# Two output buffers, one move per tile and no gate operations in the expert loop of a routed feed-forward kernel

## The reference, cut to what matters

```python
weights_BSK, indices_BSK = jax.lax.top_k(probs_BSE, TOP_K)
norm_weights_BSK = jax.nn.softmax(weights_BSK, axis=-1)
full_weights_BSE = jnp.sum(one_hot_BSKE * norm_weights_BSK[..., None], axis=2)
act_BSEF = jax.nn.silu(jnp.einsum('BSD,EDF->BSEF', x, kernel_gating_EDF))
fuse_BSEF = act_BSEF * jnp.einsum('BSD,EDF->BSEF', x, kernel_up_EDF)
down_BSED = jnp.einsum('BSEF,EFD->BSED', fuse_BSEF, kernel_down_EFD)
out_BSD = jnp.einsum('BSED,BSE->BSD', down_BSED, full_weights_BSE)
```

## Time and profile before

| | us |
|---|---|
| median of 3 runs (lowest to highest) | 2512.0 (2511.35 to 2512.2) |
| the profiled execution | 2510.75 |
| its span, first to last instruction | 2509.0 |
| TensorE busy in the span | 2347.6 |
| VectorE, ScalarE, GpSimd busy | 1589.8, 1314.9, 903.4 |
| the expert stage, from the first gather to the last scatter | 2095.22 to 2491.6 |

### The profile page before, as it was taken

How to read it: one execution, slowest core, us unless ns; L and a number is a source line. 1 busy time by engine, 2 the same in 40 slices (tenths; PEclk the granted TensorE clock), 3 DMA queues, 4 the chain that set the end, 5 groups by cost and what they waited for, 6 DMA issues and landing times. The chain is left out here.

```text
span 2509.0 us, 49491 instructions
## 1 busy us (share of the span) xinstructions
PE 2347.6 (94%) x16096; PEld 2076.7 (83%) x16096; DVE 1589.8 (63%) x3452; ACT 1314.9 (52%) x3960; POOL 903.4 (36%) x1141
## 2 busy tenths in 40 slices
PE   6999999999999999999997999999999956888895
PEld 5898889888988898889886899999999844777775
DVE  5656665666566656665655788888888855334332
ACT  4555555555555555555554666666666622333332
POOL 3233333333233323333332122222222224777774
PEclk9999999999999999999999999999999986999998
DMA  5000000000000000000001000000000012334334
GB/s 166 18 10 17 8 17 8 17 9 16 8 17 14 11 8 17 16 9 9 16 1 66 3 10 18 17 8 17 17 8 17 18 37 67 77 73 97 72 49 97
DMA packets 52931, 73.89 MB, mean 29 GB/s; under 512 B 9408, under 2 KB 36800, under 8 KB 52800
## 3 DMA queue, kind: packets, MB, share of 16 engines
q1 hardware_dynamic: 39952, 55.07, 6.9%
q0 software_dynamic: 12912, 17.98, 4.4%
HBM read 55.47 MB, written 21.76 MB: 31 GB/s over the span
## 5 line engine op out<-in xcount | busy, mean ns | idle before, releaser
L356 POOL TENSOR_TENSOR p_sb<-p_sb,rinv 128x512 f32<-128x512 f32 x256 | 284.1, 1110 | 906.3 <-DVE rinv L606 906.3
L527 ACT ACTIVATE p_sb<-s_ps,nmax 128x256 f32<-128x256 f32 x512 | 238.3, 470 | 467.1 <-DVE nmax L587 441.4
L751 POOL TENSOR_TENSOR sp_sb<-sp_sb,srinv 128x512 f32<-128x512 f32 x128 | 133.4, 1042 | 442.7 <-DVE srinv L937 442.7
L462 PE MATMUL o_ps<-pt_sb,v_sb 128*128 128x128 f32 x2048 | 270.5, 275 | 1.8 <-DVE ot_lo L57 1.8
L58 DVE SCALAR_TENSOR_TENSOR qbd_lo<-m_ps,qbd_hi 64x256 fp32r<-64x256 f32 x256 | 108.1, 422 | 227.4 <-ACT qbd_hi L46 225.7
L462 PEld LDWEIGHTS o_ps<-pt_sb,v_sb 128*128 128x128 f32 x2048 | 248.7, 192 | 2.2 <-issue 2.2
L57 DVE TENSOR_TENSOR kt_lo<-k_ps,kt_hi 128x512 fp32r<-128x512 f32 x256 | 176.2, 688 | 98.1 <-ACT kt_hi L45 94.1
L45 ACT CAST kt_hi<-k_ps 128x512 fp32r<-128x512 f32 x256 | 150.6, 588 | 105.7 <-PE k_ps L65 102.7
L885 ACT ACTIVATE sp_sb<-sm_sb,snmax 128x128 f32<-128x128 f32 x512 | 199.4, 390 | 6.6 <-DVE snmax L948 3.3
L603 DVE COPY pt_sb<-t_ps 128x512 f32<-128x512 f32 x256 | 176.4, 689 | 26.5 <-PE t_ps L449 21.8
L587 DVE TENSOR_REDUCE nmax<-s_ps 128x2 f32<-128x512 f32 x256 | 174.1, 680 | 0.0
(11 more groups left out here) (278 smaller groups left out, 7711.3 us busy)
## 6 DMA issues: line engine op xcount, KB each, us to landing
ctx_raw<-in_ctx_t SPq DMA_DIRECT2D x32, 256.0 KB, 2.8
ctx_raw<-in_ctx_t SPq DMA_DIRECT2D x64, 128.0 KB, 2.9
xn<-f_xn SPq DMA_DIRECT2D x16, 256.0 KB, 2.2
acc<-x_sb SPq DMA_DIRECT2D x16, 256.0 KB, 2.3
e_raw<-in_gate SPq DMA_DIRECT2D x8, 512.0 KB, 4.1
e_raw<-in_up SPq DMA_DIRECT2D x8, 512.0 KB, 5.0
e_raw<-in_down SPq DMA_DIRECT2D x8, 512.0 KB, 6.3
x_sb<-in_x SPq DMA_DIRECT2D x1, 3584.0 KB, 13.6
```

The lines of the kernel that those rows point to most:

```text
L356: nc.gpsimd.tensor_tensor(prob, prob, inv, ALU.mult).then_inc(norm_done, 1)
L462: mm = pe.matmul(o_ps[:, (2 * w + b) * P:(2 * w + b + 1) * P], v_sb[:, k, q * P:(q + 1) * P], pt_sb[:, w, k * P:(k + 1) * P], start=(j == ...
L527: ex = nc.scalar.activation(p_sb[:, k, b * J:(b + 1) * J], s_ps[1 - w][:, b * J:(b + 1) * J], ACT.Exp, bias=nmax[:, k, b:b + 1], scale=1.0 ...
L751: nc.gpsimd.tensor_tensor(prob, prob, inv, ALU.mult).then_inc(norm_done, 1)
```

## The change

It does four things. `e_ys` becomes `ys` with two halves, used in turn by tile parity; `y_copy(i)` waits no longer for the scatter before but for `s_out_now`, the index copy of the tile before, which GpSimd makes only when the scatter two tiles before has landed. `move` is one operation of 264 columns instead of one of 8 and one of 256, `e_xs` has 264 columns, and the 8 weights go from there to `slot_weights` by a new copy on ScalarE in `step`; `move` waits for that copy of the tile before (`s_weight`). Both gate operations are dropped; in their place stands a semaphore increment on GpSimd's queue (`pool.sem_inc(s_order, 1)`), on which nobody waits, and the waits that the gate carried are carried by it. The scatters left after the loop are written as three and a rest. The waits on a scatter between `add_rows` calls stay.

```diff
--- before.py
+++ after.py
@@ -1304,31 +1304,29 @@
         with ExitStack() as ex:
             token_now = [sbuf(ex, f"e_token_now{i}", [P, 1], mybir.dt.uint32) for i in range(2)]
             warm = sbuf(ex, "e_warm", [P, 1])
-            s_warm = sem("e_silu_table")
+            s_warm, s_ready, s_order = sem("e_silu_table"), sem("e_ready"), sem("e_pool_order")
             none = sbuf(ex, "e_none", [P, 1], mybir.dt.uint32)
-            dummy = [sbuf(ex, f"e_dummy{i}", [P, 1]) for i in range(2)]
             token_out = sbuf(ex, "e_token_out", [P, 1], mybir.dt.uint32)
             xs_in = [sbuf(ex, f"e_xs_in{i}", [P, ROW]) for i in range(2)]
-            xs_sb = sbuf(ex, "e_xs", [P, D])
+            xs_sb = sbuf(ex, "e_xs", [P, ROW])
             xt_hi = sbuf(ex, "e_xt_hi", [P, D], F32R)
             xt_lo = sbuf(ex, "e_xt_lo", [P, D], F32R)
             silu_sb = sbuf(ex, "e_silu", [P, F])
             h_sb = sbuf(ex, "e_h", [P, F])
             ht_hi = sbuf(ex, "e_ht_hi", [P, F], F32R)
             ht_lo = sbuf(ex, "e_ht_lo", [P, F], F32R)
-            ys_sb = sbuf(ex, "e_ys", [P, D])
+            ys = sbuf(ex, "e_ys", [P, 2 * D])
             xt_ps = psum(ex, "e_xt_ps")
             g_ps = psum(ex, "e_g_ps")
             u_ps = psum(ex, "e_u_ps")
             ht_ps = psum(ex, "e_ht_ps")
             y_ps = psum(ex, "e_y_ps")
-            s_now, s_moved, s_dummy = sem("e_token_now_set"), sem("e_xs_moved"), sem("e_dummy_done")
+            s_now, s_moved = sem("e_token_now_set"), sem("e_xs_moved")
             s_xs, xt_mm, xt_h, xt_l = [sem(f"e_xs_loaded{i}") for i in range(2)], sem("e_xt_mm"), sem("e_xt_hi_done"), sem("e_xt_split")
             g_mm, u_mm, silu_done, h_done = sem("e_g_mm"), sem("e_u_mm"), sem("e_silu_done"), sem("e_h_done")
             ht_mm, ht_h, ht_l = sem("e_ht_mm"), sem("e_ht_hi_done"), sem("e_ht_split")
             y_mm, y_copied, s_added = sem("e_y_mm"), sem("e_y_weighted"), sem("e_ys_added")
             s_weight, s_out_now, s_out = sem("e_weight_kept"), sem("e_token_out_set"), sem("out_stored")
-            out_gate, s_out_gate = sbuf(ex, "e_out_gate", [P, 1]), sem("e_out_gate_done")
 
             def tile_count(eng):
                 return eng.value_load(first_tile[0:1, EXPERTS:EXPERTS + 1], min_val=MIN_TILES * EXPERTS, max_val=MAX_TILES)
@@ -1378,7 +1376,7 @@
                     wait(pool, s_moved, i - 1 if isinstance(i, int) else i + -1)
                     nc.gpsimd.tensor_tensor(token_now[half][:], token_of[:, bass.ds(i, 1)], none[:], ALU.add).then_inc(s_now, 1)
                     pool.wait_ge(s_now, i + 1)
-                    nc.gpsimd.tensor_tensor(dummy[half][:], zero[:], zero[:], ALU.add).then_inc(s_dummy, 1)
+                    pool.sem_inc(s_order, 1)
                     pool.indirect_dma_start(
                         out=xs_in[half][:], out_offset=None, in_=xn_dram,
                         in_offset=bass.IndirectOffsetOnAxis(ap=token_now[half][:], axis=0)).then_inc(s_xs[half], DMA)
@@ -1386,27 +1384,24 @@
                 def move(i, pair, half):
 
                     pool.wait_ge(s_xs[half], DMA * pair + DMA)
-                    wait(pool, s_dummy, i)
-                    nc.gpsimd.tensor_tensor(weight[:, bass.ds(i * EXPERTS, EXPERTS)], xs_in[half][:, D:ROW],
-                                            zero[:].to_broadcast([P, EXPERTS]), ALU.add).then_inc(s_weight, 1)
+                    wait(pool, s_weight, i)
                     wait(pool, xt_mm, i)
-                    nc.gpsimd.tensor_tensor(xs_sb[:], xs_in[half][:, 0:D], zero[:].to_broadcast([P, D]), ALU.add).then_inc(s_moved, 1)
-
-                def add_rows(i):
+                    nc.gpsimd.tensor_tensor(xs_sb[:], xs_in[half][:], zero[:].to_broadcast([P, ROW]), ALU.add).then_inc(s_moved, 1)
+
+                def add_rows(i, half):
 
                     wait(pool, s_added, DMA * i)
                     nc.gpsimd.tensor_tensor(token_out[:], token_of[:, bass.ds(i, 1)], none[:], ALU.add).then_inc(s_out_now, 1)
+                    pool.wait_ge(y_copied, i + 1)
                     pool.wait_ge(s_out_now, i + 1)
-                    pool.wait_ge(y_copied, i + 1)
-                    wait(pool, s_out_gate, i)
-                    nc.gpsimd.tensor_tensor(out_gate[:], zero[:], zero[:], ALU.add).then_inc(s_out_gate, 1)
+                    pool.sem_inc(s_order, 1)
                     pool.indirect_dma_start(
-                        out=acc, out_offset=bass.IndirectOffsetOnAxis(ap=token_out[:], axis=0), in_=ys_sb[:],
-                        in_offset=None, compute_op=ALU.add).then_inc(s_added, DMA)
+                        out=acc, out_offset=bass.IndirectOffsetOnAxis(ap=token_out[:], axis=0),
+                        in_=ys[:, half * D:(half + 1) * D], in_offset=None, compute_op=ALU.add).then_inc(s_added, DMA)
 
                 more_pairs = pool.value_load(pairs[0:1, 0:1], min_val=MIN_TILES * EXPERTS // 2, max_val=MAX_TILES // 2)
-                nc.gpsimd.memset(none[:], 0).then_inc(s_zero, 1)
-                pool.wait_ge(s_zero, 2)
+                nc.gpsimd.memset(none[:], 0).then_inc(s_ready, 1)
+                pool.wait_ge(s_ready, 1)
                 for half in range(2):
                     gather(half, half)
                 for half in range(2):
@@ -1415,17 +1410,19 @@
                 for half in range(2):
                     move(2 + half, 1, half)
                     gather(4 + half, half)
-                add_rows(0)
+                add_rows(0, 0)
                 with pool.Fori(2, more_pairs) as j:
                     for half in range(2):
                         move(2 * j + half, j, half)
                         gather(2 * j + (2 + half), half)
-                        add_rows(2 * j + (half - 3))
+                        add_rows(2 * j + (half - 3), 1 - half)
                 for half in range(2):
                     move(2 * more_pairs + half, more_pairs, half)
-                not_added = pool.value_load(first_left[0:1, 0:1], min_val=MIN_TILES * EXPERTS - 4, max_val=MAX_TILES)
-                with pool.Fori(not_added, tile_count(pool)) as i:
-                    add_rows(i)
+                left = pool.value_load(first_left[0:1, 0:1], min_val=MIN_TILES * EXPERTS - 4, max_val=MAX_TILES - 4)
+                for k in range(3):
+                    add_rows(left + k, 1 - k % 2)
+                with pool.Fori(left + 3, tile_count(pool)) as i:
+                    add_rows(i, 0)
 
             @block.tensor
             def _(pe):
@@ -1488,6 +1485,7 @@
                     act.wait_ge(xt_mm, i + 1)
                     wait(act, u_mm, i)
                     split_hi_act(nc, xt_hi[:], xt_ps[:, 0:D]).then_inc(xt_h, 1)
+                    nc.scalar.copy(weight[:, bass.ds(i * EXPERTS, EXPERTS)], xs_sb[:, D:ROW]).then_inc(s_weight, 1)
 
                 def rest(i):
 
@@ -1502,9 +1500,8 @@
 
                 def y_copy(i, e):
                     act.wait_ge(y_mm, i + 1)
-                    act.wait_ge(s_weight, i + 1)
-                    wait(act, s_added, DMA * i)
-                    nc.scalar.activation(ys_sb[:], y_ps[:, 0:D], ACT.Copy,
+                    wait(act, s_out_now, i)
+                    nc.scalar.activation(ys[:, bass.ds((i % 2) * D, D)], y_ps[:, 0:D], ACT.Copy,
                                          scale=weight[:, bass.ds(i * EXPERTS + e, 1)]).then_inc(y_copied, 1)
 
                 def tile(i, before, e, e_before, piece):
```

## The result

| | before | after |
|---|---|---|
| median of 4 runs each, us (lowest to highest) | 2512.1 (2511.35 to 2513.57) | 2534.84 (2532.41 to 2537.5) |
| ratio (95% interval) | | 1.009 (1.0073 to 1.0107) |
| profiled execution, its span | 2510.75, 2509.0 | 2537.5, 2535.8 |

The change makes the kernel 0.9% slower. The forecast was a loss, to 2526; direction and range hold, the loss is 22.7 where 14 were forecast.

What follows compares the result with a forecast made beforehand. GpSimd's loop (5.35 us a tile) and an equally long scatter loop were taken as the bound. +3.1 +11.2 -2.4 +2.6 = +14.5 on 2510.75, plus 1.25 to the median, gave 2526 us, range 2493 to 2538.

Steps and rivals of the forecast that it cites:

- The gates: Ahead of GpSimd's transfers: the increment's wait holds the queue, exposing preparation; 1.00 us instead of 0.78 before gather, 0.95 before scatter.
- One move: In GpSimd's loop, one move of all columns takes 0.64 us instead of 0.80, -0.16 a tile.
- Two buffers: The loop from one scatter to the next becomes 5.02 us, under GpSimd's 5.44, and stops being the bound.
- the sentence on which I rested the forecast: Expert stage before: removing the scatter loop (5.34 us) alone frees nothing that GpSimd's loop (5.35) does not also free.
- The ring over ScalarE: Chain from TensorE through ScalarE's new weights copy to GpSimd's move and back: 5.15 us, hidden under GpSimd's 5.44.
- Other tiles: The 34 tile periods outside the seven weight-splitting groups: each 0.09 us longer, 5.44 against 5.35, +3.1 in all.
- slow scatters: Six scatters that meet the load of weights: each costs 0.4 us less than before, -2.4 in all.
- Groups with weights: Seven groups of four tiles round splitting the next expert's weights: VectorE's e_w_lo holds GpSimd, 1.6 us each, +11.2.
- the third piece: Third e_w_lo piece in a group of tiles that split weights: it holds token_now again, 0.85 us.
- period near 7: Sign of being right: one tile per weight-splitting group with e_xs held to 2 us or more, period near 7 us.
- The end: After the last move, four scatters: the last ends at X+17.3 us, X being the last tile's e_xt_hi start; +2.6.
- The rivals: Faster, preparation hidden: 2489 us, chance 0.22; about the same, holds not adding up: 2515, 0.16; slower, ScalarE's ring: 2532, 0.12.

## Why the prediction was right, point by point

**The gates** (forecast 1.00 and 1.00 ahead of the transfers): 1.02 and 1.03, the size is right. The mechanism was not quite the one given. It was put as "a wait that holds the queue"; the increments behind the gates carry none and give the same distances. What the runs show is that an increment between the operation that the engine still has to do and the transfer takes their overlap away, and that its place decides: ahead of the gate it costs nothing or 0.06. How it does so stays open. By the Trainium skill, Perfetto Trace Analysis, section "Sequencer-only Instruction (DRAIN, etc)", the next instruction is fetched only when such an instruction has waited, executed and pushed its update. The trace agrees where the increment carries the wait: idle time ahead of the gather is 0.83 behind it and 0.36 behind a gate. The 0.59 behind an increment that waits for nothing isn't settled by it.

**One move** (-0.16): the move ends 0.67 after the scatter's descriptors instead of 0.80, -0.13.

**Two buffers** (5.02, not a bound): in the changed kernel it is none, `e_ys` waits for TensorE only. But the sentence on which I rested the forecast is wrong, as the run with two buffers alone shows: 2499, 13 us faster. I had taken 0.95 as GpSimd's own, where 0.62 is; the second buffer was worth 0.33 a tile in GpSimd's loop. The forecast survives it by luck: it set the scatter's distance at 1.00 from a tile in which `e_ys` was late, and the increment makes it 1.03 whatever `e_ys` does.

**The ring over ScalarE** (5.15, hidden): 5.16 wherever it shows, and hidden under 5.5 in the changed kernel.

**Other tiles** (34 x 0.09 = +3.1): a common tile is 5.51, where the sum gave 5.46 and 5.44 was taken: 0.02, 0.03 and 0.03 more on the two distances and the move, some 0.03 less on the scatter and the gap behind the move. The 34 take 188.49 us instead of 182.93, +5.6. The sum has a slip here: holds and slow scatters are priced over a common tile in the groups as well, so the longer common tile belongs to all 62, not to 34. That leaves out 28 x 0.09 = 2.5, and at the measured 0.16 it is 4.5.

**Groups with weights and slow scatters** (+11.2 - 2.4 = +8.8): the 28 tiles take 187.55 instead of 167.90, +19.65. These terms were mis-sized by 10.85. `token_now` is held to 0.96 and the next move to 2.17, as described. That the third piece holds `token_now` again is so in one group only, the one without a stretch at half clock; in five of the others it meets a gather instead, which takes 1.11 to 1.17. Two timeline rows of GpSimd, from the one and from one of the others:

```profile
2205.86 1.06 POOL L1377 TENSOR_TENSOR e_token_now<-token_of,e_none 128x1 uint32<-128x1 uint32 x1 [0.18 <-POOL e_xs L1389]
...
2274.10 1.12 POOL L1380 DMA_INDIRECT e_xs_in<-xn,e_token_now  x1 [0.83 <-DMA acc<-e_ys,e_token_out]
```

The "period near 7" occurs as forecast, once, at the product that comes at 2204.03: 7.28. In the other six groups the product behind the held move came after 8.76 to 8.85, because TensorE worked at half its clock, and three of the tiles behind a slow scatter took 8.57 to 8.76 for the same reason: nine stretches. "Whose clock I assume stays at 0.99" was an assumption that broke. But 8.79 against 7.28 is not the price of a stretch, since what follows gives most of it back: the three tiles together take 7.28 + 5.48 + 6.40 = 19.16 in the group without one, and 8.79 + 5.13 + 5.62 = 19.54 in that of 2264, 19.4 to 19.6 in all six. Behind a held move a stretch costs some 0.4, since it also spares the third hold. Behind a slow scatter it costs some 1.6 (8.6 to 8.8 against 6.99 and 7.20), of which the next tile gives back 0.4.

The missing 10.85 is then, by these estimates: +4.5 for the common tile of 5.51 in the 28; +2.1 for the 0.3 that the forecast took off each of the seven groups (the group without a stretch has 19.16 - 3 x 5.51 = 2.63 of holds, where 2.6 was worked out and 2.3 used); +2.2 and +4.8 for the clock behind six moves and three scatters; -2.7 since only five slow scatters lie in these tiles, where six were counted, and for rounding. The clock's part rests on one group without a stretch. The kernel with the increments behind the gates has three such groups, with 19.15 to 19.24 for the three tiles, and four with a stretch, with 19.56 to 20.62. So behind a held move a stretch costs between 0.4 and 1.4, and the clock's exact share of the loss isn't settled.

**The end** (+2.6): X + 17.35 forecast, 17.49 from the product measured, +2.73.

Together: 5.6 + 19.65 + 2.7 = 27.9, less 1.2 by which this execution reached tile 3 earlier, is the 26.75 between the profiled executions; between the medians it is 22.7.

**The rivals.** The preparation is not hidden under the increment (distances 1.02, not 0.5). The holds do add up where all three occur. ScalarE's ring is not the bound of the changed kernel, though it is once the gates are back.

## What to carry to other kernels

A tiny operation "without use" between an index and its indirect transfer can be worth more than it costs: it carries the wait inside the engine while the transfer is made ready, 0.2 us busy for 0.2 saved ahead of the gather and 0.4 ahead of the scatter here. Before pricing a loop as an engine's own, look at its gaps in a tile in which nothing is late: a gap that contains a wait for the other loop makes two loops look equally long. And where an engine is late by two microseconds, TensorE's clock may fall behind it; price that over several tiles, since a loop that something else bounds gives part of it back.

## What the runs showed of the hardware

- A semaphore increment on GpSimd's queue, put behind a gate, makes the indirect transfer start 0.59 after the gate's end instead of 0.36 (gather), and 1.06 instead of 0.62 after the index copy (scatter). Put ahead of the gate it costs 0.06 (gather) or nothing (scatter). A second one in a row costs 0.06 to 0.15.
- TensorE idle for 2.15 us was followed, 1.4 us after it took up work, by 3.4 us at the lower of its two levels: a matmul of 512 columns 0.63 instead of 0.40. The same held move with 2.20 us idle, at the product of 2204.03, was followed by none. With the increments behind the gates, seven held moves left TensorE idle for 2.17 to 2.22 us; four were followed by such a stretch, three by none. The kernels in which no move is held have them too, one to four each and behind idle times of 1.92 to 3.11 us, except the changed kernel with `e_w_lo` in halves, which has none. What decides isn't settled by these runs.
- VectorE's `e_w_lo` of 1024 columns, with both inputs in SBUF, stretches a move of GpSimd from 0.62 or 1.2 to 2.17, and `e_token_now` from 0.19 to 0.96; in two operations of 512 columns the holds are gone or 0.44. The Trainium skill, SBUF — State Buffer, section "Who interferes with whom", says that such an instruction contends with a GpSimd instruction that reads SBUF, and calls the shared pair of ports an exclusive lock. The held times agree: `e_dummy` ends 0.06 after `e_w_lo` in the earlier trace rows, and the held move 0.47 after it.
